# Self-attention of a decoder: the projection moved between the transposes of the two heads, and the values product issued whole in every second tile

## The reference, cut to what matters

```
q, k, v = heads of layernorm(x) @ Wq, @ Wk, @ Wv       # 16 heads x 64
sim  = q @ k.T * 64**-0.5 + rel_bias                    # per batch and head, 1024 x 1024
attn = softmax(sim, axis=-1)
out  = (attn @ v) @ Wo + bo
```

## Time and profile before

| | |
|---|---|
| median of 3 runs | 2169.19 us (2168.51 to 2175.8) |
| profiled execution, device time | 2169.09 us |
| its span in the profile | 2167.3 us |
| busy over the span | PE 94%, PEld 78%, DVE 64%, ACT 48%, POOL 45% |
| tiles of the self-attention | about 50 to 902 us of the span |

### The profile page before, as it was taken

How to read it: one execution, slowest core, us unless ns; L and a number is a source line. 1 busy time by engine, 2 the same in 40 slices (tenths; PEclk the granted TensorE clock), 3 DMA queues, 4 the chain that set the end, 5 groups by cost and what they waited for, 6 DMA issues and landing times.

```text
span 2167.3 us, 54537 instructions
## 1 busy us (share of the span) xinstructions
PE 2030.5 (94%) x22465; PEld 1686.3 (78%) x22465; DVE 1392.1 (64%) x3108; ACT 1047.6 (48%) x2108; POOL 978.8 (45%) x762
## 2 busy tenths in 40 slices
PE   6999999999999999869999779999999999998994
PEld 4677777777777777558888669999989999988883
DVE  6666666666666666447887776555466455456983
ACT  3666666666666666414544444234245334324551
POOL 1555555555555555414545343433334334344441
PEclk9999999999999999969999899999999999999996
DMA  7001020101010101202131111000121010030000
GB/s 270 6 18 47 21 96 15 55 11 54 11 55 11 47 11 41 102 31 71 41 107 44 49 34 53 22 12 13 29 91 51 17 32 17 17 123 25 11 16 15
DMA packets 59990, 97.16 MB, mean 45 GB/s; under 512 B 7720, under 2 KB 50480, under 8 KB 57392
## 3 DMA queue, kind: packets, MB, share of 16 engines
q1 hardware_dynamic: 57184, 86.69, 12.0%
q10 hardware_dynamic: 2560, 6.99, 0.8%
HBM read 70.45 MB, written 23.20 MB: 43 GB/s over the span
## 4 chain that ended last, share of the span: by engine, by line
PE 42%; DVE 7%; issue 4%; ACT 2%; POOL 2%; DVEq 0%; POOLq 0%; ACTq 0%
PE psum L262 12%; PE psum L273 10%; PE psum L1814 4%; PE psum L243 2%; PE psum L1802 2%; PE psum L2306 2%; PE psum L1788 2%; PE psum L1143 1%; DVE b_act L1375 1%; PE psum L222 1%; PE psum L1130 1%; PE psum L2340 1%; DVE b_acc L1383 1%; ACT e_pr L2445 1%; POOL b_act_lo L1287 1%
## 5 line engine op out<-in xcount | busy, mean ns | idle before, releaser
L761 POOL TENSOR_TENSOR a_sm<-a_sm,a_rsum 128x1024 f32<-128x1024 f32 x256 | 485.2, 1895 | 391.2 <-DVE a_rsum L793 389.2
L781 DVE CUSTOM_DVE_ANT_0 a_sm<-psum,a_strip 128x1024 f32<-128x1024 f32 x256 | 312.0, 1219 | 57.9 <-PE psum L621 57.9
L700 ACT ACTIVATE a_sm<-a_sm,a_mn 128x1024 f32<-128x1024 f32 x256 | 293.6, 1147 | 24.2 <-DVE a_mn L781 24.1
L634 PEld LDWEIGHTS psum<-ident,a_sm 128*128 128x128 f32 x2048 | 218.9, 141 | 101.0 <-issue 92.9
L705 ACT ACTIVATE a_pT<-psum 128x512 f32<-128x512 f32 x256 | 153.0, 598 | 283.5 <-PE psum L634 283.4
L634 PE MATMUL psum<-ident,a_sm 128*128 128x128 f32 x2048 | 279.6, 280 | 4.7 <-POOL a_sm L761 4.6
L649 PE MATMUL psum<-a_pT,a_V 128*64 128x256 f32 x2048 | 249.0, 385 | 0.8 <-DVE a_pT L788 0.8
L788 DVE COPY a_pT<-psum 128x512 f32<-128x512 f32 x256 | 176.3, 689 | 101.5 <-PE psum L634 101.5
L649 PEld LDWEIGHTS psum<-a_pT,a_V 128*64 128x64 f32 x2048 | 136.2, 136 | 77.3 <-issue 21.1
L1898 ACT ACTIVATE g_val<-psum 128x512 f32<-128x512 f32 x64 | 38.1, 597 | 219.4 <-PE psum L1814 219.4
L1287 POOL TENSOR_TENSOR b_act_lo<-b_act,b_act_hi 128x512 fp32r<-128x512 f32 x64 | 91.2, 1430 | 102.2 <-ACT b_act_hi L1185 102.2
(11 more groups left out here) (329 smaller groups left out, 4234.4 us busy)
## 6 DMA issues: line engine op xcount, KB each, us to landing
a_strip<-table SPq DMA_DIRECT2D x16, 960.0 KB, 6.5
oT<-a_o SPq DMA_DIRECT2D x64, 128.0 KB, 1.9
b_oT_in<-oT SPq DMA_DIRECT2D x8, 1024.0 KB, 5.5
a_raw<-in_a_wqkv SPq DMA_DIRECT2D x7, 384.0 KB, 3.3
s_x<-in_x_rev SPq DMA_DIRECT2D x4, 512.0 KB, 7.4
vb<-s_zero SPq DMA_DIRECT2D x8, 256.0 KB, 2.7
b_x_in<-in_x SPq DMA_DIRECT2D x8, 256.0 KB, 5.6
b_vb_in<-vb SPq DMA_DIRECT2D x8, 256.0 KB, 5.4
```

The costliest lines, as they stand in the source:

```text
L634: last = pe.transpose(psum[:, 4 + j, k * P:(k + 1) * P], sm[:, st % RING, kt * P:(kt + 1) * P], ident[:, :])
L700: a.activation(sm[:, st % RING, :], sm[:, st % RING, :], ACT.Exp, scale=-1.0, bias=mn[:, at:at + 1], accum_out=rsum[:, at:at + 1]).then_in ...
L761: g.tensor_tensor(sm[:, st % RING, :], sm[:, st % RING, :], rsum[:, at:at + 1].broadcast_to([P, T]), ALU.mult).then_inc(sig("scaled"), 1)
L781: v.tensor_tensor_reduce(out=sm[:, st % RING, :], in0=scores_banks(hl).rearrange("p c n -> p (c n)"), in1=strip[:, pair % 2, hl, qt * P:qt ...
```

## The change

In PE's order of a tile, `project` goes ahead of the second head's transposes. The values of a group are no longer split over an even and an odd tile: both halves are issued in the even tile, after the second head's transposes, and the odd tile has none. The work, the buffers and every other engine's order stay. 

```
                     transposed(n, 0)
-                    if n > 1:
-                        values(n // 2 - 1, n % 2)
-                    transposed(n, 1)
                     if NU + n < len(units):
                         project(NU + n)
+                    transposed(n, 1)
+                    if n > 1 and n % 2 == 0:
+                        values(n // 2 - 1, 0)
+                        values(n // 2 - 1, 1)
                 values(NG - 1, 0)
                 values(NG - 1, 1)
```

## The result

| | before | after |
|---|---|---|
| median of 4 runs | 2172.49 us (2168.51 to 2183.25) | 2202.01 us (2200.09 to 2209.04) |
| profiled execution, device time | 2169.09 us | 2203.24 us |
| its span | 2167.3 us | 2201.4 us |
| busy over the span | PE 94%, DVE 64%, ACT 48%, POOL 45% | PE 92%, DVE 63%, ACT 47%, POOL 44% |

The changed kernel is slower: the ratio of its time to that of before is 1.0136, with an interval of 1.0115 to 1.0158. The forecast was 2197 us with a range of 2182 to 2213.

What follows compares the result with a forecast made beforehand. The prediction took PE to set the pace, with a chain of 6.89 us close behind. Steady part +21.2, last block +8.3 and first tiles -2 gave +27.5 us on 2169.09, say 2197 us, range 2182 to 2213.

Steps and rivals of the forecast that it cites:

- chain of 6.89 us: From a tile's scores through DVE's reads and POOL's first-head scaling until that head's transposes can begin: 6.89 us, unchanged by PE's order.
- The saved changes of tiling: In PE's order over two V tiles, fewer array tiling changes: 12.31 us of PE work against 12.78, saving 0.47 a pair.
- The odd tile: Without values, PE waits for DVE before the next scores (4.83 us), then for POOL before first-head transposes (6.89 us).
- The even tile: From 6.89 us, unhindered 6.37 with a V unit or 6.88 with q or k, plus small waits in second transposes.
- wait for bank 5: Even tile's second transposes wait for DVE's copy after an odd q or k tile: +0.20 us with an even V unit.
- The split: DVE's 1.41 us weight split in one odd tile of sixteen delays bank 5's copy: +0.62 us a q, V pair, 7 times.
- The last block: Tiles without projections: pairs take 13.35 us against 11.04, 3 times, plus 1.4 for tiles 119 and 120: +8.3 us.
- First tiles: At the start, projections fit into PE's 1.94 us wait for POOL, and the clock loss may go: -2 us, bounds -3 and 0.
- The 21.2 us of the steady pairs: Sum of the forecast changes over all kinds of pairs in the steady part of the self-attention: +21.2 us.
- The first, no waits: Rival: throughout the attention, tiling drains are saved and nothing waits, 63 pairs x 0.47 = 30 us, 2139 us; chance 0.06.
- The second, larger savings: Rival: waits come, but tiling changes save about 0.3 us more a pair, 19 off, 2178 us, no change; chance 0.08.
- The third, a fallen clock: Rival: PE's gaps lower the clock; last block +7, about 2204 us; steady part 49 more, 2246 and above, chance 0.06.

Runs made afterwards that it cites:

- first edit alone: Kernel before with only the projection moved ahead of the second head's transposes, each values half after them in its own tile: 2158.89 us, ratio 0.9936.
- split moved: Changed kernel with DVE's split of the weights moved from the end of an odd tile to the end of the even tile after it: 2196.03 us, ratio 1.0092.
- second edit alone: Kernel before with a group's whole values product in the even tile, between the two heads' transposes, projection still last: 2215.72 us, ratio 1.0183.
- half scale, changed kernel: Changed kernel with POOL scaling only the first 512 of a head's 1024 columns: 2178.99 us, ratio 1.0019 to the kernel before.
- half scale, kernel before: Kernel before with POOL scaling only half of each head's columns, as a control: 2169.83 us, ratio 0.9973.

## Why the prediction was right

**What bounds the kernel.** The pace was set by PE with a chain of 6.89 us close behind. After the change the chain shows at 6.88 in the pairs read above, bare, and PE waits for it. That the chain would not stretch or shrink with PE's new order was right to 0.01 us.

**The saved changes of tiling.** Costed at 0.47 us a pair. The first edit alone saves 0.27 (12.79 to 12.52), where its two turns were costed at 0.32. The whole product of 3.60 us (428.13 to 431.73) against the costed 3.59 was right. The saving is real and is kept in the even tile, and lost in the waits of the odd one. The Trainium skill's rule (TensorEngine Tiling (Array Packing), Key Properties: a change of tiling mode drains the engine) agrees with the first edit alone, where a tile has three changes instead of four and takes 6.27 us instead of 6.39. It did not decide the outcome.

**The odd tile.** Two waits, scores at 4.83 and transposes at 6.89: measured 4.83 and 6.88. Halving POOL's work moved the second and not the first.

**The even tile.** V, V, V, k and k, q pairs came within 0.01. The wait for bank 5 in q, V pairs is there, and with it the pair was costed 0.07 too high.

**The split.** Here part of the mechanism was wrong, and not only the size: +0.62 a pair forecast, +1.06 measured, 7 times. I had carried the split's 1.41 us over from a place where it meets 0.59 us of POOL's work to one where it meets 1.21. And I had let it delay the copy of bank 5, where it is the second head's reciprocal, and through it POOL, that came late: the second transposes of the even tile start 9.75 us after the odd tile's scores. That they would start more than 9.3 us after them was named as a sign that the forecast is wrong, and in these 7 pairs of the 63 it came true.

**The last block.** +8.3 forecast, +5.8 measured. The pairs after tile 119, 121 and 123 grew by 1.44, 2.30 and 2.54. I had counted a third full pair, at tile 125; but its even tile issues the last scores, and from those of tile 125 to the cross-attention the time fell by 0.5 us.

**First tiles.** -2 forecast, -1.0 measured. The scores of tile 3 came 2.8 us earlier (66.17 instead of 68.97): the projection now lies within the wait for POOL, of which 1.28 us are left, and the clock was 1.00 from 66 to 70 us, where it had been 0.57. But the pair after tile 1 takes 15.38 us, against 15.49, as its even tile now holds the whole of the first group's values, 3.61 us (71.31 to 74.92), where it had half. With the first edit alone that pair takes 13.65. The forecast had left this half out at the start, and its absence in tile 127 at the end.

The misses, +2.5 for the q, V pairs, -2.5 for the last block and +1 for the first tiles, largely cancelled, so that the sum of 27.5 is so close to 27.9 is in part luck. The 21.2 us of the steady pairs stand on their own: they measured 23.1.

**The rivals.** The first, no waits, fell with the first 4.83 and 6.88. The second, larger savings, fell with pairs of 13.36, which leave room for 0.01; the weight loads of the scores that had waited start with their matmuls, at 423.20, and not ahead of them. The third, a fallen clock, did not come in the attention: 1.00 from 100 to 850 us, and on to 932, in the last block too.

## What to carry to other kernels

When one engine is busy throughout, measure the chain of the others beside it from its own start to where it is needed, and compare it with the time that the busy engine takes to come there. Work that is moved from one iteration to the next leaves the sum as it is and takes the cover away: a loop whose iterations are unequal is set by the chain in the short one and by its work in the long one. Here bundling the values product took a pair of V tiles from 12.52 us, with the projection's move alone, to 13.36; the move, which kept the iterations equal, was the gain.

## What the hardware showed that was not expected

DVE's split, a tensor-tensor operation on two SBUF operands, has a duration that follows POOL's work: 1.40 us where it overlaps 0.59 us of it (before), 2.02 with 1.21 (after), 2.28 with 1.47 (split moved, and second edit alone), 1.18 with 0.37 (half scale, changed kernel), and 0.95 with none (half scale, kernel before). The longest is shown above, with the split moved; the shortest:

```profile
402.38 0.95 DVE L814 TENSOR_TENSOR a_W<-a_raw,a_W 128x768 fp32r<-128x768 f32 x1
```

Wherever it overlaps, POOL was already scaling when the split began, and the split ends 0.81 us after POOL's step: until then it stands still. POOL's step keeps its 1.90 us. DVE's reading of the scores, with one operand in PSUM, keeps its 1.22 us beside POOL. The Trainium skill states this in SBUF — State Buffer, Who interferes with whom: a DVE operation with both inputs in SBUF waits for the read port that it shares with GpSimd, held for the whole instruction. These traces agree, with the numbers above. No step of POOL began while a split was running, so whether POOL would then stand still was not seen here.
